# Mixture-of-experts routing on VectorE and TensorE: bf16 comparison tables, one masked scan, owners turned early, and a later request for the third tile's weights

## What is computed

```python
        def _moe_mlp(x, gate_w, gate_b, w1, w2):
            logits = xf @ gate_w + gate_b
            one_hot = jax.nn.one_hot(jnp.argmax(logits, axis=-1), E, dtype=xf.dtype)
            h = jax.nn.gelu(jnp.einsum('td,edh->teh', xf, w1), approximate=True)
            y = jnp.einsum('teh,ehd->ted', h, w2)
            out = jnp.einsum('te,ted->td', one_hot, y)
        x = x + _moe_mlp(_layernorm(x, ln2_w, ln2_b), gate_w, gate_b, w1, w2)
```

## Time and profile before

| | us |
|---|---|
| median of 3 runs | 1586.13 |
| lowest, highest | 1585.42, 1589.29 |
| the profiled execution | 1584.35 |
| its span, first to last instruction | 1582.4 |
| TensorE busy | 1473.8 |
| VectorE busy | 1141.2 |
| ScalarE busy | 877.6 |
| GpSimd busy | 378.8 |

### The profile page before, as it was taken

One profiled execution on the slowest core, in us unless ns is written; L12 is line 12 of the kernel. 1 busy time (PEld: TensorE's weight loads), 2 busy tenths in 40 slices (PEclk: granted clock), 3 DMA queues, 4 the chain that ended last, 5 costly groups with the idle time before them and its releaser, 6 DMA issues. The chain is left out here.

```text
span 1582.4 us, 44773 instructions
## 1 busy us (share of the span) xinstructions
PE 1473.8 (93%) x18524; PEld 1077.7 (68%) x18524; DVE 1141.2 (72%) x1711; ACT 877.6 (55%) x1606; POOL 378.8 (24%) x601
## 2 busy tenths in 40 slices
PE   7997899977899999999999999999999759999997
PEld 4654677654445666666666666666658649999997
DVE  5787698877868889898988989888846643333332
ACT  2223566654447888888888888888884211111111
POOL 4110332223431111111111111111101024444443
PEclk9998899999999999999999999999999769999999
DMA  6000000002331111111111111111106745656562
GB/s 201 1 21 21 1 2 2 2 1 80 130 138 38 40 39 36 42 36 41 38 39 37 39 41 36 42 37 40 40 6 204 233 159 188 215 186 215 188 210 69
DMA packets 80082, 124.10 MB, mean 78 GB/s; under 512 B 22244, under 2 KB 46950, under 8 KB 79879
## 3 DMA queue, kind: packets, MB, share of 16 engines
q1 hardware_dynamic: 74262, 105.87, 22.2%
q0 software_dynamic: 5616, 15.34, 2.6%
HBM read 94.66 MB, written 26.08 MB: 76 GB/s over the span
## 5 line engine op out<-in xcount | busy, mean ns | idle before, releaser
L548 DVE TENSOR_REDUCE sb_m_mx<-banks 128x1 f32<-128x1024 f32 x512 | 603.4, 1219 | 77.7 <-PE banks L307 69.7
L470 ACT ACTIVATE sb_m_pT<-banks 128x512 f32<-128x512 f32 x1024 | 556.3, 594 | 111.6 <-PE banks L336 100.5
L336 PE MATMUL banks<-sb_m_q,sb_m_k 99*32 99x512 bf16 x4096 | 467.9, 380 | 2.3 <-DMA sb_m_q<-sb_m_mx_parts 1.3
L307 PE MATMUL banks<-sb_m_k,sb_m_q 96*32 96x512 bf16 x4096 | 360.5, 379 | 1.5 <-DMA sb_m_k<-k_parts 1.0
L351 PE MATMUL banks<-sb_m_pT,sb_m_v 128*32 128x256 f32 x4096 | 315.1, 378 | 0.7 <-ACT sb_m_pT L470 0.7
L336 PEld LDWEIGHTS banks<-sb_m_q,sb_m_k 99*32 99x32 bf16 x4096 | 177.8, 95 | 82.2 <-ACT sb_m_pT L470 6.1
L351 PEld LDWEIGHTS banks<-sb_m_pT,sb_m_v 128*32 128x32 f32 x4096 | 175.9, 109 | 60.2 <-ACT sb_m_pT L470 1.2
L307 PEld LDWEIGHTS banks<-sb_m_k,sb_m_q 96*32 96x32 bf16 x4096 | 158.2, 96 | 77.4 <-DVE sb_m_mx L548 5.6
L2437 ACT ACTIVATE sb_e_hT<-banks 128x512 f32<-128x512 f32 x78 | 46.6, 597 | 237.6 <-PE banks L2397 237.6
L228 POOL CAST sb_m_mx_parts<-sb_m_mxT 8x128 bf16<-8x128 f32 x64 | 18.2, 284 | 575.6 <-issue 564.0
L2397 PEld LDWEIGHTS banks<-sb_e_xT,w 128*128 128x128 f32 x1248 | 147.9, 195 | 4.3 <-DVE sb_e_xT L2447 2.4
(11 more groups left out here) (243 smaller groups left out, 1894.3 us busy)
## 6 DMA issues: line engine op xcount, KB each, us to landing
w<-in_w SPq DMA_DIRECT2D x47, 1024.0 KB, 5.2
sb_m_q<-q_parts SPq DMA_DIRECT2D x384, 32.0 KB, 1.8
sb_m_k<-k_parts SPq DMA_DIRECT2D x384, 32.0 KB, 1.8
q_parts<-sb_m_parts SPq DMA_DIRECT2D x24, 256.0 KB, 2.4
k_parts<-sb_m_parts SPq DMA_DIRECT2D x24, 256.0 KB, 2.4
X<-in_x SPq DMA_DIRECT2D x4, 1024.0 KB, 10.0
x_rows<-X SPq DMA_DIRECT2D x8, 512.0 KB, 9.2
z_rows<-sb_g_zs SPq DMA_DIRECT2D x8, 512.0 KB, 5.0
```

The source lines that it names most:

```text
L307: mm = pe.matmul(ps[2 * (k % 2) + h][c:c + 32, :], q_s[0:R, i, k * P + c:k * P + c + 32], k_s[0:R, i, h * 512:(h + 1) * 512], start=True, ...
L336: mm = pe.matmul(ps[rotating(use)][c:c + 32, :], k_s[:, i2, m * P + c:m * P + c + 32], q_s[:, i2, h * 512:(h + 1) * 512], start=True, stop ...
L470: act.activation(pT[:, m, h * 512:(h + 1) * 512], ps[rotating(f"b{m}{h}")][:, :], ACT.Exp).then_inc(exped, 1)
L548: dve.tensor_reduce(mx[:, par % 2, k:k + 1], pz[:, 2 * (k % 2):2 * (k % 2) + 2, :].rearrange("p q n -> p (q n)"), AX.X, ALU.max).then_inc( ...
```

## The change

In `route`:

- All two-dimensional tables are laid out with the experts (or blocks, or places) outside and the 32 groups of tokens inside; before it was the other way round for most. `logits` keeps its layout, so it is read across.
- The eight prefix sums after the counting become one masked scan ahead of it: `going_on` is 1 and, at the first group of every expert, 0, so that one pass over 8 x 32 elements restarts for each expert. TensorE then sums the scan over the partitions and adds, in the same bank, a product of `hot` with `before` less ones. The totals are asked for first, as a product of 8 columns.
- The number of blocks is got by adding 127 and shifting, on 8 elements, where a comparison and a reduce over 256 stood. The owners are found one to a partition (8 elements each), and turned into one row by a product on TensorE.
- What depends only on the token's number (`left`, its two bytes, the spare slots' numbers) is computed while TensorE counts. The two bytes are of 4096 less the token's number; a slot that no token has gives 0.
- ScalarE makes bf16 copies of the constants (`block_starts`, `places`), GpSimd makes `before_less` and `going_on`. The comparisons and products that build the tables (`at_block`, `left_at`, `at_place`) have bf16 inputs and outputs, and `left_at` is made in four pieces beside those of `at_place`. TensorE's 32 products now read both tables with a step of 32 elements.
- After these products there are six steps where five stood.
- SP issues two w1 loads instead of three. The third is issued at the start of `experts`, after the first gathered rows have landed (`z_in[0]`).

The core of the diff:

```diff
         def _(sp):
-            sp.wait_ge(owner_done, 1)
-            for j in range(len(w1_in)):
+            sp.wait_ge(owner_done, 2)
+            for j in range(len(w1_in) - 1):
...
         def _(pe):
-            flat = hot[:, :, :].rearrange("p n e -> p (n e)")
-            pe.matmul(ps[0][:, 0:NT * E], before[:, :], flat, start=True, stop=True).then_inc(counted, 1)
-            pe.matmul(ps[1][:, 0:NT * E], every[:, :], flat, start=True, stop=True).then_inc(counted, 1)
+            pe.matmul(ps[0][:, 0:E * NT], before_less[:, :], hot[:, :, :].rearrange("p e n -> p (e n)"),
+                      start=True, stop=False)
+            pe.wait_ge(hot_done, 2)
+            pe.matmul(ps[1][:, 0:E], every[:, :], until[:, :, NT - 1], start=True, stop=True).then_inc(counted, 1)
+            pe.matmul(ps[0][:, 0:E * NT], every[:, :], until[:, :, :].rearrange("p e n -> p (e n)"),
+                      start=False, stop=True).then_inc(counted, 1)
+            pe.wait_ge(owner_done, 1)
+            pe.matmul(ps[3][0:1, 0:J], owner_col[:, :], ident[:, 0:J], start=True, stop=True).then_inc(counted, 1)
             for n in range(NT):
-                mm = pe.matmul(ps[2][:, 0:2 * J], at_place[:, n, :], less_at[:, n, :, :].rearrange("p r j -> p (r j)"),
+                mm = pe.matmul(ps[2][:, 0:2 * J], at_place[:, :, n], left_at[:, :, :, n].rearrange("p q j -> p (q j)"),
                                start=(n == 0), stop=(n == NT - 1))
...
+        def _(act):
+            act.activation(block_starts[:, :, :], count[:, 0:J].unsqueeze(2).broadcast_to([P, J, NT]),
+                           ACT.Identity, scale=float(P)).then_inc(tables_made, 1)
+            act.activation(places[:, :, :], count[:, :].unsqueeze(2).broadcast_to([P, P, CH]),
+                           ACT.Identity).then_inc(tables_made, 1)
...
+            dve.tensor_tensor_scan(until[:, :, :].rearrange("p e n -> p (e n)"), going_on[:, :, :].rearrange("p e n -> p (e n)"),
+                                   hot[:, :, :].rearrange("p e n -> p (e n)"), 0.0, ALU.mult, ALU.add).then_inc(hot_done, 1)
...
-            for e in range(E):
-                sc = dve.tensor_tensor_scan(until[:, e, :], every[:, 0:NT], total[:, e, :], 0.0, ALU.mult, ALU.add)
...
+            ch.link(dve.scalar_tensor_tensor(out=place[:, :, :], in0=over_n(base[:, :]), scalar=float(P),
+                                             in1=ps[0][:, 0:E * NT].rearrange("p (e n) -> p e n", e=E),
+                                             op0=ALU.mult, op1=ALU.add))
...
-            for q in range(2):
-                last = dve.tensor_tensor(less_at[:, :, q, :], at_block[:, :, :],
-                                         part[:, q, :].unsqueeze(2).broadcast_to([P, NT, J]), ALU.mult)
             for n in range(0, NT, CH):
-                dve.tensor_tensor(at_place[:, n:n + CH, :], count[:, :].unsqueeze(1).broadcast_to([P, CH, P]),
-                                  in_block[:, n:n + CH].unsqueeze(2).broadcast_to([P, CH, P]),
+                dve.tensor_tensor(left_at[:, :, :, n:n + CH], at_block[:, :, n:n + CH].unsqueeze(1).broadcast_to([P, 2, J, CH]),
+                                  part[:, :, n:n + CH].unsqueeze(2).broadcast_to([P, 2, J, CH]), ALU.mult)
+                dve.tensor_tensor(at_place[:, :, n:n + CH], places[:, :, :],
+                                  in_block[:, n:n + CH].unsqueeze(1).broadcast_to([P, P, CH]),
                                   ALU.is_equal).then_inc(at_done, 1)
...
+            e = sp.value_load(owner[0:1, ds(W - 1, 1)], min_val=0, max_val=E - 1)
+            sp.wait_ge(z_in[0], 16)
+            sp.dma_start(w1[:, W - 1, :, :], dram["w1"][ds(e, 1), :, :].rearrange("o (k p) n -> p (o k) n", p=P)).then_inc(
+                w1_in[W - 1], 16)
             for j in range(W, J):
                 load(j, j % W)
```

More of the change, by code:

```diff
@@ L2143, in sem @@
         return ctx.enter_context(nc.semaphore("r_" + name))
[L2145 removed]
+    ps, ident, logits, owner, token_from, token_to = (t[n] for n in (
+        "ps", "ident", "logits", "owner", "token_from", "token_to"))
     E = dram["gate_w"].shape[1]
     J = dram["slot"].shape[1]
[L2148 to L2149 removed]
+    before, prefer, count, token, slot_no = (t["tables"][n] for n in ("before", "prefer", "count", "token", "slot"))
     w1, w1_in, tables_in = t["w1"], t["w1_in"], t["tables_in"]
     TABLES = 16 * len(t["tables"])
+    CH = 8
     every = sb("every", [P, P])
+    before_less = sb("before_less", [P, P])
+    going_on = sb("going_on", [P, E, NT])
     best = sb("best", [P, NT])
[L2154 removed]
+    hot = sb("hot", [P, E, NT])
     rank = sb("rank", [P, NT])
[L2156 to L2157 removed]
+    ranked = sb("ranked", [P, E, NT])
     until = sb("until", [P, E, NT])
     place = sb("place", [P, E, NT])
[L2160 removed]
+    total_i = sb("total_i", [P, E], I32)
+    blocks_i = sb("blocks_i", [P, E], I32)
     blocks = sb("blocks", [P, E])
@@ L2163, in route @@
     base = sb("base", [P, E])
+    reached = sb("reached", [P, E])
+    owner_col = sb("owner_col", [P, 1])
     row = sb("row", [P, NT])
     row_i = sb("row_i", [P, NT], I32)
-    block_i = sb("block_i", [P, NT], I32)
     in_block_i = sb("in_block_i", [P, NT], I32)
[L2168 to L2171, removed]
+    in_block = sb("in_block", [P, NT], BF16)
+    block_at = sb("block_at", [P, NT], BF16)
+    left = sb("left", [P, NT])
+    left_i = sb("left_i", [P, NT], I32)
     part_i = sb("part_i", [P, 2, NT], I32)
[L2173 to L2177, removed]
-    found = sb("found", [P, J])
[L2179 to L2185, removed]
+    part = sb("part", [P, 2, NT], BF16)
+    own_slot = sb("own_slot", [P, J])
+    places = sb("places", [P, P, CH], BF16)
+    block_starts = sb("block_starts", [P, J, NT], BF16)
+    at_block = sb("at_block", [P, J, NT], BF16)
+    left_at = sb("left_at", [P, 2, J, NT], BF16)
+    at_place = sb("at_place", [P, P, NT], BF16)
+    low = sb("low", [P, J])
+    found = sb("found", [P, J])
+    spare_slot = sb("spare_slot", [P, J])
+    moved = sb("moved", [P, J])
+    ones_set, tables_made, owner_done, hot_done, counted, steps, at_done, found_done = (sem(n) for n in (
+        "ones_set", "tables_made", "owner_done", "hot_done", "counted", "steps", "at_done", "found_done"))
+    assert B * S + J * P < 1 << 16 and J <= P and B * S <= 256 * 256
     with nc.Block() as block:
@@ L2246, in _ @@
[L2246 to L2251, removed]
@@ new lines, in _ @@
+            ch.link(dve.tensor_scalar(blocks_i[:, :], total_i[:, :], P.bit_length() - 1, None, ALU.logical_shift_right))
+            ch.link(dve.tensor_copy(blocks[:, :], blocks_i[:, :]))
+            ch.link(dve.tensor_tensor_scan(blocks_until[:, :], every[:, 0:E], blocks[:, :], 0.0, ALU.mult, ALU.add))
+            dve.tensor_scalar(reached[:, :], blocks_until[:, :], token[:, 0:1], None, ALU.is_le)
+            ch.link(dve.tensor_tensor(base[:, :], blocks_until[:, :], blocks[:, :], ALU.subtract))
@@ L2293, in experts @@
+            dve.tensor_scalar(token_from[:, :], moved[:, :], float(B * S), float(B * S - 1), ALU.add, ALU.min)
+            ch.link(dve.tensor_scalar(token_to[:, :], moved[:, :], float(B * S), None, ALU.add))
 def experts(nc, ctx, t, dram):
```

82 lines of the change are left out of this document (41 added, 41 removed).

## The result

| | before | after |
|---|---|---|
| median of 5 runs, us | 1586.13 | 1578.58 |
| lowest, highest | 1584.13, 1589.29 | 1574.70, 1581.03 |
| ratio of the runs | | 0.9947, 95% interval 0.9925 to 0.9968 |
| profiled execution, its span | 1584.35, 1582.4 | 1578.58, 1576.5 |

The ratio is 8.4 us of 1586, its interval 5.1 to 11.9 us; the two medians differ by 7.55. Two windows of the changed kernel, columns as in the earlier trace rows. The routing is 16.10 us long instead of 23.80. VectorE is busy for 13.28 us of it, the same share as before (19.61 of 23.80), and TensorE for 7.61 instead of 4.85. The expert stage is as before.

A forecast was written before the change was run, and what follows sets the result against it. TensorE sets the expert stage's pace; the routing before it is a serial prelude, mostly on VectorE, whose savings shorten the whole. Its terms summed to -8.7 us, giving 1577.4 us against the median 1586.13, range 1574.2 to 1583.0.

The forecast's parts named there:

- finding the expert: Routing's first five VectorE instructions, two now reading their input across: +0.34 us, with +0 as the other end.
- counting: VectorE's wait for TensorE's count, now ending in a pair of 8 columns instead of 256: -0.50 us.
- count to multiplication: VectorE from the count to the row of each token, 5.72 us before and 1.69 after: -4.03 us.
- multiplication, reduce, owners: VectorE's multiplication, reduce read across and owners' step, 1.18 us where 1.08 stood: +0.10 us.
- small steps: VectorE's small instructions before the tables, ten taking 1.79 us, now four linked taking 0.87: -0.92 us.
- first table: VectorE's 1248-element table instruction, at half the time per element with bf16, starts its successor after 0.84 us: -0.65 us.
- four rounds: VectorE's four rounds of table building at bf16 pace, 4.09 us instead of 7.36: -3.27 us.
- TensorE behind the last comparison: TensorE's last eight products at the tables and VectorE's wait for them, said to stay at 0.80 us: change 0.
- tail: VectorE's steps after TensorE's products, six where five stood, four linked at 0.23 us: +0.25 us.
- the bf16 terms: Table building on VectorE with bf16 inputs at two elements a cycle: first table -0.65 us, four rounds -3.27 us.
- rival B: TensorE slows at the tables, reading elements 64 bytes apart: +3.4 us, leaving -5.3 and 1580.8 us; chance 0.13.
- Rival D: Expert stage gives gain back: gather meets weight loads or third tile waits; -5.6, 1580.5 us; chance 0.06.

The follow-up runs named there:

- e5: Changed kernel with three small table operands float32 again instead of bf16; last comparison ends 17.02 us after the routing's start against 12.93; single execution 1584.55 us.
- e7: Changed kernel with the old block count (256 elements) and owners in one partition; first turn 21.82 us after the routing's start against 20.68; single execution 1582.46 us.
- e3: Changed kernel with only TensorE's weights table at 4-byte steps, moving operand still 64; 0.134 us a pair against 0.148, third tile at 35.87 us against 36.12.
- e4: Changed kernel with only TensorE's moving operand at 4-byte steps, weights still 64; 0.070 us a pair against 0.148, third tile at 35.62 us against 36.12.
- e6: Changed kernel with the third w1 load issued in the routing again; first turn 3.16 us after the gather's issue against 3.31, third tile at 35.80 against 36.12.
- e1: Changed kernel with both tables TensorE reads at 4-byte steps instead of 64; 0.063 us a pair against 0.148, third tile at 35.29 us against 36.12.

## Why the prediction was right

It forecast 1577.4 us and -8.7; the median is 1578.58 and the ratio gives -8.4. By its steps, measured from the same rows (the tail here to the end of its last step):

| step | predicted | measured |
|---|---|---|
| finding the expert | +0.34 | +0.45 |
| counting | -0.50 | -0.70 |
| count to multiplication | -4.03 | -4.05 |
| multiplication, reduce, owners | +0.10 | +0.11 |
| small steps | -0.92 | -0.93 |
| first table | -0.65 | -0.65 |
| four rounds | -3.27 | -3.29 |
| TensorE behind the last comparison | 0 | +1.17 |
| tail | +0.25 | +0.26 |
| sum, routing | -8.7 | -7.6 |

Right, and shown by a run of its own: the bf16 terms, together -3.94 (e5 gives back 4.09), and, of the -4.05 from the count to the multiplication, the 1.3 us of the blocks and the owners (e7). Right by the rows alone: the rest of that step, where the prefix sums left the chain, both reads across (0.62 and 0.59 us where L2258 had shown 0.59), the small steps, and the cover of ScalarE's and GpSimd's new work.

Wrong was one step: "TensorE's last eight products and their wait ... stay at 0.80". The pairs slowed from 0.063 to 0.148 us, past the 0.125 that a round of VectorE covers. That is rival B's mechanism at a smaller size: B priced a pair at 0.22 from float32 weight loads and the end at +3.4 us, and it was +1.17. B also named the weights and the moving columns together; the moving ones alone do nearly all of it (e3, e4). Two of the prediction's signs came out on B's side: the pairs are not at 0.06 us, and TensorE is busy without a break while VectorE waits at the end.

Two things outside the sum came on top. The gather took 3.31 us to the first turn instead of 3.14 (+0.17), and the first 32 products took 5.46 us instead of 6.40 (-0.94). The windows over these 32 products, before and after, have granted clocks of 0.58 and 0.69: both start at 0.50, and the clock rose earlier in the second.

```profile
1287.68:1294.08 6.40, 6.40 (x34) 6.38 (x34) 0.00 (x0) 0.60 (x1) 3.06 (x4) 0.58 0.33 95
```

```profile
1282.75:1288.21 5.46, 5.46 (x34) 5.44 (x34) 0.00 (x0) 0.60 (x1) 2.88 (x4) 0.69 0.82 298
```

The prediction put this at 0, give or take a microsecond. So that the total came within 0.3 us of -8.7 is luck: a miss of +1.17 on TensorE was nearly made up by a term put at 0. How much of the -0.94 belongs to the change is open. In the nine profiles of the changed order with no extra products the 32 products took between 5.19 and 6.36 us, so that much of it is chance; but all nine lie under the 6.40 of the kernel before, of which there is only one profile. Without it the change would be worth some 7.5 us, which would still have been within the range.

Rival D was given 0.06 and had no share. The prediction's reason for moving the third load, to keep it off the gather, did not matter here: in e6 the load's traffic was almost over when the gather's rows moved. Its "cost 0" for the move holds, and the gain is 0 too. The scan took 0.69 us, between the 0.43 and 1.03 of the bounds. It was not wholly in idle time, since TensorE's next weight load waited 0.16 us for it:

```profile
1263.96 0.69 PEld L2218 LDWEIGHTS banks<-sb_r_until,sb_r_every 128*128 128x128 f32 x2 [0.16 <-DVE sb_r_until L2258]
```

## What to carry to other kernels

When two engines share a table, ask of each layout what the reader pays as well as the writer: the layout that gave VectorE its halved time made TensorE the later one, and neighbours in pairs would have served both better (e1 reads the product 0.9 us sooner). A serial prelude can be summed instruction by instruction from its own rows: here each step came out within 0.2 us, but for the one whose new access pattern no row had, which was off by 1.17. And where code ahead of a change drifts by several microseconds from run to run, measure from the changed stage's own start.

## What was not expected

- TensorE's moving operand is read at 0.148 us for 78 columns when each element lies in 16 bytes of its own, at either level of its clock.
- The masked scan over 256 elements took 0.69 us, where other passes over 256 take 0.42. Less the 0.15 us that the prediction took off each instruction, that is twice the time per element.
- L2253, a multiplication over 256 elements whose neighbour L2255 took 0.43, took 0.51 us instead of 0.42, while GpSimd's difference of 128 columns ran beside it for 0.80, longer than its 256-column ones of 0.72. It took 0.51 us in the profiles of all the experiments too. ScalarE's new passes are not the reason: in e1 they had ended 0.55 us before it began. Whether it and GpSimd slow each other was not tested.
- Asking for the third tile's weights early did not delay the gather (e6): the load's traffic was nearly over when the gather's rows began to move.
